# A four-layer graph network on one core: weights applied ahead of the two hop sweeps, masks counted in four column quarters

## The reference, cut to what matters

```python
# layer 0
Ax = adj @ h
x += 1 - 0.1 * h - 0.01 * sum(h * Ax, axis=1)
# layer 1, two hops
for k in range(2):
    h = tanh(concat([adj @ h, h], axis=1) @ W[k])      # W[k]: 128 x 64
x += h
# layer 2: of the nonzero entries of a row only the last 100 count, halving from the last back
mask = adj != 0; rank = cumsum(mask, axis=1); ...
x += w @ (h @ weight) + bias
# layer 3
u_intra = tanh([h, t] @ W1 + b1) @ W2 + b2
x += u_intra + adj @ (h @ B.T) - rowsum(adj) * (h @ B.T)
```

## Time and profile before

| | |
|---|---|
| median of 3 runs | 762.15 us (760.29 to 762.63) |
| profiled execution | 756.76 us, its span 755.0 us |
| busy in the span | PE 699.3 us, DVE 446.5 us, ACT 183.1 us, POOL 103.2 us |
| moved by DMA | 262.58 MB, 348 GB/s in the mean |

### The profile page before, as it was taken

One profiled execution on the slowest core, in us unless ns is written; L12 is line 12 of the kernel. 1 busy time (PEld: TensorE's weight loads), 2 busy tenths in 40 slices (PEclk: granted clock), 3 DMA queues, 4 the chain that ended last, 5 costly groups with the idle time before them and its releaser, 6 DMA issues. The chain is left out here.

```text
span 755.0 us, 10045 instructions
## 1 busy us (share of the span) xinstructions
PE 699.3 (93%) x3642; PEld 279.3 (37%) x3656; DVE 446.5 (59%) x765; ACT 183.1 (24%) x271; POOL 103.2 (14%) x126
## 2 busy tenths in 40 slices
PE   1899899998989999999999997999899989999997
PEld 0333333333333333444444443444344433333332
DVE  5766676777888878846665556688788740000000
ACT  2010111100100000101111113888788832000010
POOL 5011011111100000001222222011111121211210
PEclk9899999999999999999999999999999999999999
DMA  9999999996699999699998986699999839999994
GB/s 369 374 366 415 415 420 414 413 412 242 250 395 408 329 374 388 260 375 377 364 372 317 368 319 217 244 405 337 341 366 370 302 128 348 372 407 410 364 398 167
DMA packets 49680, 262.58 MB, mean 348 GB/s; under 512 B 6880, under 2 KB 18912, under 8 KB 19296
## 3 DMA queue, kind: packets, MB, share of 16 engines
q1 hardware_dynamic: 39136, 252.51, 85.8%
q10 hardware_dynamic: 10496, 9.44, 4.0%
HBM read 255.76 MB, written 6.16 MB: 347 GB/s over the span
## 5 line engine op out<-in xcount | busy, mean ns | idle before, releaser
L1144 PE MATMUL accA<-land,X 128*64 128x512 f32 x1504 | 363.0, 600 | 8.6 <-DMA land<-adj_blocks 7.7
L1144 PEld LDWEIGHTS accA<-land,X 128*64 128x64 f32 x1504 | 100.9, 137 | 183.8 <-issue 140.9
L1144 PE MATMUL accA<-cache,X 128*64 128x512 f32 x544 | 133.3, 601 | 17.4 <-DVE X L1009 12.6
L958 DVE TENSOR_TENSOR uS<-uS,land 128x512 f32<-128x512 f32 x186 | 130.6, 702 | 30.5 <-DMA land<-adj_blocks 20.9
L976 DVE TENSOR_SCALAR uS<-land 128x1024 bf16<-128x1024 f32 (+1 forms) x188 | 125.8, 720 | 38.0 <-DMA land<-adj_blocks 37.1
L481 ACT ACTIVATE wS<-spare 128x1024 uint16<-128x1024 f32 x112 | 108.2, 1033 | 31.1 <-PE spare L1176 30.4
L1176 PE MATMUL spare<-uS,triA 128*128 128x512 bf16 x247 | 74.8, 382 | 15.5 <-DVE wS L479 11.4
L638 POOL TENSOR_TENSOR hS<-tS 128x256 f32<-128x256 f32 x24 | 21.2, 883 | 425.7 <-DVE tS L839 425.7
L942 DVE TENSOR_TENSOR tS<-uS,nat 128x256 f32<-128x256 f32 x8 | 3.4, 422 | 122.9 <-PE nat L1076 122.9
L1187 PE MATMUL accA<-wS,X 128*128 128x512 bf16 x251 | 75.4, 381 | 0.4
L1144 PEld LDWEIGHTS accA<-cache,X 128*64 128x64 f32 x544 | 38.7, 138 | 91.0 <-issue 83.3
(11 more groups left out here) (83 smaller groups left out, 388.2 us busy)
## 6 DMA issues: line engine op xcount, KB each, us to landing
land<-adj_blocks SPq DMA_DIRECT2D x219, 1024.0 KB, 7.1
cache<-adj_blocks SPq DMA_DIRECT2D x17, 1024.0 KB, 13.6
xin<-x_rows ACTq DMA_DIRECT2D x32, 128.0 KB, 7.5
x_rows<-zS ACTq DMA_DIRECT2D x24, 128.0 KB, 4.8
cache<-x_rows SPq DMA_DIRECT2D x1, 1024.0 KB, 4.9
uS<-counts SPq DMA_DIRECT2D x64, 4.0 KB
out_rows<-zS ACTq DMA_DIRECT2D x8, 128.0 KB, 6.2
rows_transposed<-rowsT SPq DMA_DIRECT2D x7, 128.0 KB, 6.6
```

Of the source, the lines that this page charges most:

```text
L958: nc.vector.tensor_tensor(total, total, of[:, i * W:(i + 1) * W], ALU.add)\
L1144: last = nc.tensor.matmul(accA[k * D:(k + 1) * D, c % 2, :], tile(X[p % 2], TQ * q + k), of[:, k * W:(k + 1) * W], start=(b == 0), stop=(b ...
```

## The change

1. The hops multiply by W ahead of the sweep. When a chunk's rows h are ready (in L0 for the first hop, in L1A for the second), PE turns them ("turn"), and a new step "hop" multiplies them by both halves of W[k] at once: h @ W_upper are the rows to sweep (in `X`), h @ W_lower the rows to add (in `Z`, which takes the space of `wS`). "wx" and "agg" go; `accS` is transposed in L1A and L1B as in L3, DVE adds the two halves and `Z` (`hop_added`), and ACT applies tanh to the result.
2. Masks are counted in four column quarters: tile t goes to partitions 32 (t mod 4) and on, through a 32-column slice of `later`. ACT copies all 128 partitions (`partS`), and a matmul "stack" with a stack of unit matrices adds up the four quarters. Counts and left weights have 32 rows instead of 64.
3. L0, L1A and L1B get stage tables of their own, and the stages of the counts are spread over the chunk.

```diff
-HT_PE = {L1B: "turn", L2: 7}
+HT_PE = {L0: "turn", L1A: "turn", L1B: "turn", L2: 7}
+STAGES_L0 = {0: 1, 1: 2, "part": 3, 3: 5, "stack": 5, "counts": 6, 4: 7, 5: 8, "weights": 8, 6: 10, "left": 10, 7: 11,
+             "left out": 12, "turn": 13, "turned": 13, "hop": 14, "hopped": 15}
+STAGES_L1A = {1: 2, "added": 4, "tanh": 6, "turn": 8, "turned": 9, "hop": 11, "hopped": 13}
+STAGES_L1B = {0: 1, 1: 3, "added": 5, "tanh": 6, 3: 7, 4: 8, 5: 10, "turn": 12, "turned": 13, 6: 15, 7: 15}
-QUICK = {L1A: {0: 0, 1: 1, 3: 4, 4: 5, 5: 6, 6: 7, 7: 9}, L1B: {0: 0, 1: 1, 3: 4},
+QUICK = {L1A: {0: 0, 1: 1, 3: 3, 4: 4, 5: 5, 6: 7, 7: 8, "turn": 9, "turned": 9, "hop": 10, "hopped": 11, "part": 12,
+               "stack": 12, "counts": 13, "weights": 13, "left": 14, "left out": 15},
+         L1B: {1: 1, "added": 2, "tanh": 3, "turn": 5, "turned": 5, "hop": 7, "hopped": 8},
...
 ACT
+                if at == "tanh":
+                    act.wait_ge(nat_evac, nat_no(p, c, 0) + 1)
+                    nc.scalar.activation((hS if p == L1A else natS)[:, :], tS[:, :], ACT.Tanh).then_inc(tanh_done, 1)
+                if at == "hopped":
+                    act.wait_ge(hop_done, hop_no(p, c) + 1)
+                    for of, to in ((0, X[1] if p == L0 else X[0]), (1, Z)):
+                        nc.scalar.activation(chunk(to, ch(p, c)).rearrange("p (b t d) -> p b t d", b=2, d=D),
+                                             hop_out(of), ACT.Copy).then_inc(hop_evac, 1)
+                    if p in (L0, L1A):
+                        act.wait_ge(left_made, min(c + 1, NC - 1) if p == L0 else NC)
-                    nc.scalar.activation(upperS, spare[D:P, c % 2, :], ACT.Copy).then_inc(count_half, 1)
+                    nc.scalar.activation(partS[:, :], spare[:, c % 2, :], ACT.Copy).then_inc(parts_out, 1)
...
 DVE
+                def hop_added():
+                    dve.wait_ge(nat_done, nat_no(p, c, 0) + 1)
+                    dve.wait_ge(hop_evac, 2 * hop_no(p - 1, ch(p - 1, ch(p, c))) + 2)
+                    parts = nat[:, :].rearrange("p (t h d) -> p h t d", h=2, d=D)
+                    L(nc.vector.tensor_tensor(rows4(tS), rows4(chunk(Z, ch(p, c))), parts[:, 0], ALU.add))
+                    nc.vector.tensor_tensor(rows4(tS), rows4(tS), parts[:, 1], ALU.add).then_inc(nat_evac, 1)
-                        nc.vector.tensor_tensor(countS, upperS, spare[0:D, c % 2, :], ALU.add).then_inc(count_ready, 1)
+                        nc.vector.tensor_copy(countS[0:NT, :], spare[0:NT, c % 2, :]).then_inc(count_ready, 1)
...
 PE
-                if at == 0 and p in (L1A, L1B):
-                    transposed(lambda j: tile(X[p % 2], 4 * ch(p, c) + j))
-                            nc.tensor.matmul(nat_pair(j), rows_t(j), wt(f"wx{k}"), start=(j == 0), stop=False)
-                            last = nc.tensor.matmul(nat[:, j * D:(j + 1) * D], accS[:, j * P:(j + 1) * P],
-                                                    wt(f"wagg{k}"), start=False, stop=(j == 3))
+                        if p in (L1A, L1B, L3):
                             last = nc.tensor.transpose(nat[:, j * P:(j + 1) * P], accS[:, j * P:(j + 1) * P],
+                if at == "hop":
+                    for t in (0, 2, 1, 3):
+                        half = (t // 2 * D, t // 2 * D + D)
+                        last = nc.tensor.matmul(spare[:, 2 + t // 2, t % 2 * P:(t % 2 + 1) * P],
+                                                rows_t(t % 2)[half[0]:half[1], :],
+                                                wt("hop0" if p == L0 else "hop1", rows=half), start=True, stop=True)
+                    last.then_inc(hop_done, 1)
+                if at == "stack":
+                    nc.tensor.matmul(spare[0:NT, c % 2, :], later[:, 2 * NT:3 * NT], partS[:, :],
+                                     start=True, stop=True).then_inc(stacked, 1)
...
                 for k in range(TQ):
                     t = TQ * b + k
-                    last = nc.tensor.matmul(spare[k * D:(k + 1) * D, c % 2, :], later[:, 2 * (NT - t):2 * (2 * NT - t)],
-                                            masks(b)[:, k * W:(k + 1) * W], start=(b == 0), stop=(b == NQ - 1))
+                    g = t % 4 * NT
+                    last = nc.tensor.matmul(spare[g:g + NT, c % 2, :], later[:, NT - t:2 * NT - t],
+                                            masks(b)[:, k * W:(k + 1) * W], start=(t < 4), stop=(t >= NT - 4))
```

More of the change, by code:

```diff
@@ L164, in copied_no, with tr_no @@
     return {L0: c, L1B: 8 + 2 * c + i, L2: 24 + c, L3: 32 + c}[p]
-def tr_no(p, c, i=0):
-    return {L1A: c, L1B: 8 + 2 * c + i, L2: 24 + c, L3: 32 + c}[p]
+def tr_no(p, c):
+    return {L0: c, L1A: 8 + c, L1B: 16 + c, L2: 24 + c}[p]
 TOTALS = {L1A: (1, 2, 3, 4, 7, 9, 10, 11, 12, 15), L1B: (0, 5, 6, 8, 13, 14)}
@@ L187, in totalled_no, with hop_no, tanh_no @@
     return (first - 1) * c + at - 1 if p == L1A else (first - 1) * NC + second * c + at
+def hop_no(p, c):
+    return {L0: c, L1A: 8 + c}[p]
+def tanh_no(p, c):
+    return {L1A: c, L1B: 8 + c}[p]
 def row_no(p, c):
@@ L475, in weights_out @@
                 eng.wait_ge(w_used, n - WRING + 1)
+            else:
+                eng.wait_ge(nat_evac, nat_no(L1B, 2 * n + 1) + 1)
             k = b % 2
@@ L751, in epilogue @@
                         act.wait_ge(hT_out, 16 * c)
-                    act.wait_ge(tr_done, tr_no(p, c, 1 if p == L1B else 0) + 1)
+                    act.wait_ge(tr_done, tr_no(p, c) + 1)
+                    if p in (L0, L1A):
+                        act.wait_ge(left_made, min(c + 1, NC - 1) if p == L0 else NC)
                     rows_transposed()
@@ L777, in epilogue @@
                     act.dma_start(chunk(rows_to[p], ch(p, c)), zS[:, :]).then_inc(rows_out, 16)
-                if p == L0 and at == 4:
+                if at == "part":
                     act.wait_ge(counted, NQ * (c + 1))
                     if c:
-                        act.wait_ge(count_ready, c)
-                    nc.scalar.activation(upperS, spare[D:P, c % 2, :], ACT.Copy).then_inc(count_half, 1)
-                if p == L0 and at == 7:
-                    act.wait_ge(count_ready, c + 1)
[L785 to L790, removed]
+                        act.wait_ge(left_made, c)
+                        act.wait_ge(hop_done, hop_no(L0, c - 1) + 1)
+                    if c == NC - 1:
+                        act.wait_ge(hop_done, hop_no(L0, c) + 1)
+                    nc.scalar.activation(partS[:, :], spare[:, c % 2, :], ACT.Copy).then_inc(parts_out, 1)
+                if at == "weights":
+                    act.wait_ge(count_ready, c + 1)
+                    act.dma_start(counts_d[c], countS[0:NT, :]).then_inc(counts_out, 16)
+                    act.wait_ge(stacked, c + 1)
+                    nc.scalar.activation(lomostS, countS[0:NT, :], ACT.Relu, bias=wt("full", rows=(0, NT)),
+                                         scale=-BIT).then_inc(left_most, 1)
+                if at == "left out":
                     act.wait_ge(left_made, c + 1)
@@ L1049, in epilogue @@
                 p, c = e
-                if at == 0 and p in (L1A, L1B):
-                    tr_free(tr_no(p, c, 0))
-                    transposed(lambda j: tile(X[p % 2], 4 * ch(p, c) + j))
                 if at == ("sums" if p == L3 else 1):
-                    nat_free(nat_no(p, c, 0))
                     if p == L1B:
                         pe.wait_ge(totalled, totalled_no(L1B, c, totals_at(L1B, c)[-1]))
+                        tr_free(tr_no(p, c))
                         if c:
@@ L1083, in epilogue @@
                 if at == HT_PE.get(p, None):
-                    tr_free(tr_no(p, c, 1 if p == L1B else 0))
-                    pe.wait_ge(h_ready, row_no(p, c) + 1)
+                    tr_free(tr_no(p, c))
+                    if p == L1A:
+                        pe.wait_ge(tanh_done, tanh_no(p, c) + 1)
+                    else:
+                        pe.wait_ge(h_ready, row_no(p, c) + 1)
                     transposed(lambda j: tile(hS, j))
@@ L1123, in rows_ready_for @@
                         pe.wait_ge(x_ready, part // 2)
-                elif p == L1A:
-                    pe.wait_ge(h_ready, row_no(L0, part) + 1)
+                elif p in (L1A, L1B):
+                    pe.wait_ge(hop_evac, 2 * hop_no(p - 1, ch(p - 1, part)) + 1)
                 else:
-                    pe.wait_ge(nat_evac, (nat_no(L1A, ch(L1A, part)) if p == L1B else nat_no(L2, ch(L2, part), 1)) + 1)
+                    pe.wait_ge(nat_evac, nat_no(L2, ch(L2, part), 1) + 1)
             def main(p, c, b, before):
@@ L1205, in step @@
                     pe.wait_ge(count_ready, NC)
+                    pe.wait_ge(hop_evac, 2 * hop_no(L1A, NC - 1) + 2)
                 if s >= 2:
```

136 lines of the change are left out of this document (68 added, 68 removed).

## The result

The changed kernel takes 775.43 us (median of 4 runs, 774.88 to 775.99), the kernel before 761.92 us beside it: ratio 1.0188, 95% interval 1.0158 to 1.0219. It is slower. The profiled span is 773.0 us against 755.0.

The account below looks back on a forecast made before the run. Loads were taken to bound L0, PE L1A and L1B. L0 +28.4, boundary 0, L1A -0.7 and +1.0, L1B -9.3, L2 -0.5 sum to +18.9 us on 762.15: 781 us, range 764 to 800.

Parts of the forecast that it names:

- The price of the shape: In L0, each change of tile shape costs PE 0.148 us; 32 more changes a chunk make 4.74 us.
- the weight load of 32 columns: At L0's counts, a 32-column weight load could only spare some of the second part of the price, about 0.05 us.
- +28.4: L0 turns from load-bound to PE-bound, 24.2 us a chunk against the loads' 21.3, and gets 28.4 us longer.
- rival 3: A full drain at each shape change: 0.215 us each, 6.9 us a chunk in L0, 798 us in all; chance 5%.
- Work moved into L0: Per L0 chunk, turn 0.43 us, hop 0.44 and stack 0.215 add 1.09 us of PE time.
- the wait for the left entries: In L0, DVE's "left" at block 10 waits for left_adj: costs nothing with PE as bound; uncovered, 4 us a chunk.
- Rival 1: Quarters cost nothing beside halves: loads still hide L0's PE work, L1B decides, -9 us, 753 us, faster; chance 15%.
- The forecast's sign: The whole kernel gets slower, 781 us against 762.15, 2.5%; chance of slower 82%.
- 16% for faster: The chance given to the whole kernel measuring faster, beside 82% for slower and 2% for within 0.3%.
- L0 to L1A: At this boundary a slower first L1A chunk gives the starved second its time back: net 0, from -3 to +3 us.
- L1A and L1B: L1A: -0.7 us, and +1.0 for later loads. L1B: chunks of 16.6 us, loads covered at 395 GB/s, -9.3 us.
- the 4 us allowed for late slots: In L1A, DVE's two added adds release landing slots later: +1.0 us for later loads, range 0 to +4.

Follow-up runs that it names:

- Experiment 2: Kernel before with only the counts changed to 32-column slices in four column quarters (counts not right): 771.20 us, ratio 1.0192.
- experiment 1: Changed kernel with counts in 64-column halves and a 64-column stack; hop, turn and stack stay in L0: 764.44 us, ratio 1.0056.
- 5: Changed kernel with counts in column halves, plus the left entries' load issued after the next chunk's fourth load, not all eight: 756.37 us, ratio 0.9946.
- experiment 7: Changed kernel with only the left entries' load issued earlier, after the next chunk's fourth load: 779.06 us, ratio 1.0245.
- experiment 4: Changed kernel with DVE's additions for adj's row sums taking 64 of each 512 columns, except the first in each chunk: 766.78 us, ratio 1.0118.
- experiment 8: Changed kernel with column halves, earlier left-entries load, and turn moved later in L1A's first chunk (with stages behind it) and in L1B: 752.50 us, ratio 0.9910.

## Why the prediction was right, point by point

**The price of the shape.** The forecast took 0.148 us for each change and measured are 0.13: 0.10 and 0.11 ahead of the first matmul, 0.05 in the sweep behind, and at most 0.01 in the count itself (395 ns in the mean, 385 before). The one part that was put in doubt beforehand, the weight load of 32 columns, is the one that isn't there. So a chunk pays 32 x 0.13 = 4.2 us instead of 4.74, and L0 +24.1 instead of +28.4. Experiment 2 shows the price alone, 1 and 5 its removal. The Trainium skill's "TensorEngine Tiling (Array Packing)", Key Properties, warns that changing the mode drains TensorE, and gives no size. These runs agree that a change costs time. The prediction's estimate of a full drain was 0.165 us ahead of the first matmul; 0.10 to 0.11 are measured, so rival 3 falls.

**Work moved into L0.** 1.09 us were forecast. Turn adds 0.44 us, the stack 0.22, and from the hop to the next sweep there are 0.65 us, of which 0.22 belong to its changes of shape; the hop's row halves run side by side (eight records in 0.71 us). That is 1.09 us. Right.

**Cost nothing: the wait for the left entries.** In the changed kernel that was right, and its reason too (landing in 5.1 us; in experiment 7 the earlier load doesn't shorten L0). What was wrong is the sentence on the other case, "two pairs already issued behind it keep the queue fed, and PE catches up": with the loads as the bound the wait costs L0 9.5 us (183.3 against 173.8 in experiments 1 and 5). Over seven chunks that is 1.4 us a chunk, less than the 4 us that the prediction named for that case. Rival 1 was therefore mispriced: with a block of 1.075 us, as this rival had it, the kernel came out at a ratio of 1.0056 (experiment 1), slower than before, and not at the 0.988 of its 753 us. The forecast's sign didn't hang on it, its 16% for faster did.

**L0 to L1A.** Net 0 was forecast, +0.5 is measured (first two chunks 37.0 us against 36.5), though with larger parts: PE waits 2.78 us in turn, and the clock falls behind it. The window of the whole chunk has a granted clock of 0.92. The timeline shows a turn of 1.07 us where others take 0.66, and the window under it a clock of 0.50, which is 1.2 GHz, where PE had waited just before:

```profile
220.52 0.29 DVE L883 TENSOR_SCALAR hS<-tS 128x256 f32<-128x256 f32 x1 [0.86 <-POOL tS L665]
...
220.96 1.07 PE L1089 MATMUL tr<-wts,hS 128*64 128x128 f32 x8 [2.78 <-DVE hS L883]
221.75 1.98 PE L1194 MATMUL accA<-land,X 128*64 128x512 f32 x4
```

```profile
222.00:223.00 1.00, 1.00 (x5) 0.05 (x1) 0.86 (x3) 0.38 (x1) 0.00 (x0) 0.50 0.97 410
```

By 225 us the clock is back at 1.00. The second chunk, which starved before, gave nearly all of it back (15.8 us instead of 19.7), as said.

**L1A and L1B.** PE's periods were right to 0.01 us: L1A's is 15.70, and L1B's 16.59 in the chunks of experiments 4 and 8 where PE waits for nothing. In the changed kernel itself L1B's chunks took 16.9 us or more from the second on. L1A came out at +2.1 instead of +0.3, within the 4 us allowed for late slots, and experiment 4 shows that cause. L1B is the mis-sized term: -4.9 us instead of -9.3. The forecast set 395 GB/s against the 422 of the best window, which is one of L1A, and took the loads for covered; they aren't, chunk by chunk. L1B's own window before already had a DMA share of 0.99 at 370 GB/s, so there was less room to count on than it seemed, although later chunks did reach 394 and 398 GB/s at the same share. A part is turn's wait for the norm, which the forecast left out; moving turn takes it away and doesn't shorten L1B (experiment 8). That the sum came out within 1 us is luck, as the errors cancel: -4.3 in L0, +1.8 in L1A, +4.4 in L1B and -2.9 in L2 and L3, so that +18.9 us met +18.0 in the spans. The medians, 775.43 and 761.92, are 13.5 apart: the profiled execution of before lay 5.2 us below its median, that of after (774.88) 0.5. The forecast had added its difference to the median of before, hence 781.

## What to carry to other kernels

Give small matmuls between large ones the large ones' tile shape, or let them stand together: here two counts of the wrong shape cost 0.26 us beside 0.215 us of streaming, and four of them cost no more. When a stage's bound changes, every wait that it covered has to be priced again; here a 64 KB load issued behind eight of 1 MB was free at one bound and cost 9.5 us at the other. Work taken off one engine's path in L1B, where the loads had 7% of room by the best window, gave back half of it: 4.9 us of 9.3.

## What the runs showed that was not expected

A change of shape costs nearly the same ahead of its first matmul whatever the pair: 0.09 to 0.11 us between 128*64, 128*32, 128*128 and 64*128, in either direction. What it adds in that matmul differs: 0.01 us or less in the count, 0.05 in the sweep and in the f32 join (1.05 to 1.10), and 0.10 in the hop, whose second pair of records starts 0.21 us behind the first where the others are 0.105 apart. The counts are both bf16 and only 32 columns wide, so which of the two spares them is not shown.

The traces also show that the weights don't load ahead over a change of shape. In the changed kernel the count's weight load starts with the count itself:

```profile
60.81 0.10 PEld L1210 LDWEIGHTS spare<-uS,later 128*32 128x32 bf16 x2 [0.81 <-issue]
60.81 0.40 PE L1210 MATMUL spare<-uS,later 128*32 128x512 bf16 x2
```

In the kernel before, with one shape, the sweep's weights start 0.21 us ahead of it:

```profile
45.26 0.36 PEld L1144 LDWEIGHTS accA<-land,X 128*64 128x64 f32 x4 [0.31 <-issue]
45.47 0.60 PE L1144 MATMUL accA<-land,X 128*64 128x512 f32 x2
```

It is so at every change of shape in both kernels: there the weight load starts 0.03 us ahead of its matmul at most, where within the shape 128*64 it starts 0.43 us ahead in the median. How much of the 0.10 us is this load and how much something else, no run separates.
